# Delta-rule phase: order of conv taps, norms, solve rows, projections and grams inside an iteration

## The reference, cut to what matters

```
x = x + attn_b(layernorm(x))

q, k, v = silu(causal_conv(h @ q_w)), silu(causal_conv(h @ k_w)), silu(causal_conv(h @ v_w))   # 4 taps per channel
beta = sigmoid(h @ b_w);  g = sigmoid(h @ mix_w + mix_b + mix_bias)
q, k = l2norm(q), l2norm(k);  v = v * beta;  kb = k * beta
attn = where(strictly lower, -(kb @ k.T), 0)              # per chunk, 32 x 32
for i in 1 .. 31:  attn[i, :i] += attn[i] @ attn          # solve of a triangular system, row by row
T = attn + I;  u = T @ v;  w = T @ kb
for each chunk:                                           # the chain over the state S
    u = u - w @ S
    o = q @ S + where(lower, q @ k.T, 0) @ u
    S = S + k.T @ u
o = g * o + (1 - g) * v
o = o * rsqrt(mean(o * o) + eps) * o_norm_w
out = o @ o_w
```

## Time and profile before

| | us |
|---|---|
| three runs | 2082.21, 2083.87, 2087.22 |
| median | 2083.87 |
| the profiled execution's own time | 2075.59 |
| its span in the trace | 2073.9 |
| iterations i = 1 to 6 (2 to 5 hold all five stages, 1 no tail, 6 no tile to load) | 63.3, 68.8, 63.4, 64.8, 65.8, 60.3 |
| VectorE / TensorE / ScalarE busy, iteration 1566.7 to 1631.5 | 48.3 / 48.3 / 33.0 |

### The profile page before, as it was taken

The page is one execution under the profiler, slowest core; times in us unless marked ns, Lnnn a source line. Parts: engine busy times, 40 slices in busy tenths (PEclk is TensorE's granted clock), DMA queues, the critical chain, the costliest instruction groups (busy, mean ns, idle before and its releaser), DMA issues. The chain is left out here.

```text
span 2073.9 us, 33664 instructions
## 1 busy us (share of the span) xinstructions
PE 1227.0 (59%) x13780; PEld 588.4 (28%) x13780; DVE 1440.7 (69%) x1745; ACT 915.5 (44%) x1681; POOL 1108.7 (53%) x527
## 2 busy tenths in 40 slices
PE   4356556655555655553476464577777777637655
PEld 2112112121211212120133221244544445423322
DVE  3799899999989999999661123676697667536102
ACT  5556564746556474554122205443455444213220
POOL 1879798798979888899511001234442344440100
PEclk8676767777676777765689877777788787768877
DMA  4828183462818356281289972122212222148997
GB/s 124 190 50 193 32 198 78 124 151 52 195 28 201 74 132 133 52 190 34 79 351 373 386 292 54 31 53 63 59 40 60 66 61 64 43 120 356 368 395 275
DMA packets 195624, 301.87 MB, mean 146 GB/s; under 512 B 84176, under 2 KB 126672, under 8 KB 179088
## 3 DMA queue, kind: packets, MB, share of 16 engines
q1 hardware_dynamic: 190656, 297.26, 48.8%
q0 software_dynamic: 2304, 2.37, 0.5%
q10 hardware_dynamic: 2512, 0.10, 0.1%
HBM read 257.21 MB, written 42.47 MB: 145 GB/s over the span
## 5 line engine op out<-in xcount | busy, mean ns | idle before, releaser
L361 POOL TENSOR_TENSOR state<-dx_rep,b_rep 128x2048 f32<-128x2048 f32 x128 | 578.1, 4521 | 120.4 <-PE psum L729 93.4
L591 DVE TENSOR_TENSOR_SCAN psum<-psum,state 128x1024 f32<-128x1024 f32 x160 | 365.2, 2282 | 29.5 <-ACT psum L472 18.0
L472 ACT ACTIVATE psum<-delta_rep,a_neg 128x511 f32<-128x511 f32 x512 | 331.4, 684 | 67.7 <-DVE state L591 67.6
L729 PE MATMUL psum<-state,sel 128*32 128x512 f32 x1024 | 181.7, 812 | 199.0 <-POOL state L370 185.8
L660 PE MATMUL psum<-xt,w_in 128*128 128x512 f32 x256 | 180.2, 870 | 154.8 <-DVE x_conv L560 52.1
L591 DVE TENSOR_TENSOR_SCAN state<-psum,state 128x1024 f32<-128x1024 f32 x96 | 218.8, 2280 | 19.1 <-ACT psum L472 19.1
L370 POOL TENSOR_TENSOR state<-state,c_rep 128x1024 f32<-128x1024 f32 x96 | 225.4, 2348 | 0.6 <-DVE state L591 0.6
L598 DVE TENSOR_TENSOR state<-psum,c_rep 128x1024 f32<-128x1024 f32 x160 | 195.9, 1224 | 5.5
L856 POOL DMA_DIRECT2D moe_b<-in_w x64 | 33.0, 522 | 254.1 <-DVE moe_xt L1007 253.5
L469 ACT COPY psum<-zeros 128x2 f32<-128x2 f32 x160 | 26.2, 164 | 281.0 <-DVE state L598 276.2
L660 PEld LDWEIGHTS psum<-xt,w_in 128*128 128x128 f32 x256 | 69.1, 283 | 272.4 <-issue 124.7
(11 more groups left out here) (214 smaller groups left out, 2509.9 us busy)
## 6 DMA issues: line engine op xcount, KB each, us to landing
moe_w_set<-in_w SPq DMA_DIRECT2D x32, 4096.0 KB, 37.3
delta_rep<-delta_scratch SPq DMA_DIRECT2D x128, 256.0 KB, 5.3
dx_rep<-dx_scratch SPq DMA_DIRECT2D x128, 256.0 KB, 8.0
b_rep<-bc_scratch SPq DMA_DIRECT2D x32, 256.0 KB, 4.8
delta_scratch<-delta SPq DMA_DIRECT2D x32, 256.0 KB, 4.2
dx_scratch<-delta_x SPq DMA_DIRECT2D x32, 256.0 KB, 3.8
c_rep<-bc_scratch SPq DMA_DIRECT2D x32, 256.0 KB, 7.9
moe_x<-x_after SPq DMA_DIRECT2D x16, 512.0 KB, 10.6
```

Of the source, the lines that this page charges most:

```text
L361: nc.gpsimd.tensor_tensor(ring[q % RING][:, :, :], dx_rep[u % CHUNKS][:, :, :], free_bcast(b_rep[q // QPB % 2][:, g, :], 1, CB), ALU.mult) ...
L472: ins = nc.scalar.activation(dec[:, i, 1:], delta_rep[u % CHUNKS][:, c, 1:], ACT.Exp, scale=a_neg[:, dt * CB + c, g:g + 1])
L591: nc.vector.tensor_tensor_scan(bx if by_pool(k) else flat, flat, bx, 0.0, ALU.mult, ALU.add).then_inc(S["scan_done"], 1)
L729: ins = nc.tensor.matmul(bank[32 * c:32 * c + 32, :], sel[:, :], ring[q % RING][:, c, :], start=False, stop=(g == NG4 - 1), skip_group_che ...
```

## The change

It moves steps between slots on VectorE, ScalarE and TensorE. No instruction is added or taken away but waits; the programs of SP and GpSimd are untouched.

- The first projection of a unit and its `last_tap` leave the last slot of one iteration for the first of the next; TensorE's six projections stand in slots 0, 1, 2, 2, 4, 5.
- VectorE's taps run in pairs behind the three state copies; `bn_stats` and `bn_aggr` move from slot 3 to slot 0; `o_ms` from 3 to 2; the shift from 5 to 4. Solve rows 1 to 5, 6 to 9, 10 to 12 and 13 to 15 stand at slots 3, 5, 7 and 8. The residual add moves from 7 to 8.
- ScalarE's output and layer norms go one slot ahead, the four norms activations from slot 7 to 4; `ot_delta`, `silu`, `squares` one slot back.
- TensorE's outputs, statistics, `turn_rows` and tokens go one slot back; the grams from 12 and 14 to 13 and 14, with the masks behind each. For the first unit the grams stand ahead of the tokens (11, 12 and then 13, 14).

The core of the diff:

```diff
+        def token_slots(f):
+            return (13, 14) if f == 0 else (11, 12)
+        def gram_slots(f):
+            return (11, 12) if f == 0 else (13, 14)
...
# ScalarE
-                        if front is not None and m < 5:
-                            last_tap(f, m + 1)
-                        if tail is not None and m == 2:
+                        if front is not None and m < NT:
+                            if f == 0 and m == 0:
+                                act.wait_ge(S["conv_loaded"], 16 * 3)
+                            last_tap(f, m)
+                        if tail is not None and m == 1:
                             act.wait_ge(S["o_added"], tail + 1)
...
-                        if tail is not None and m == 4:
+                        if tail is not None and m == 3:
                             act.wait_ge(S["o_ms"], tail + 1)
...
-                        if conv is not None and m == 4:
+                        if conv is not None and m == 3:
                             act.wait_ge(S["ln_mv"], CT * (a + 1))
...
+                        if conv is not None and m == 4:
+                            act.wait_ge(S["ln_shift"], a + 1)
+                            for n_ in range(CT):
+                                ins = nc.scalar.activation(x[:, n_, :], x[:, n_, :], ACT.Identity, bias=nmr[:, n_:n_ + 1],
+                                                           scale=rstd[:, n_:n_ + 1])
+                            ins.then_inc(S["ln_done"], 1)
-                        if tail is not None and m == 5:
+                        if tail is not None and m == 6:
...
-                        if conv is not None and m == 7:
-                            act.wait_ge(S["ln_shift"], a + 1)
...
-                        if front is not None and m == 11:
-                            for n_ in range(CT):
+                        if front is not None and m in token_slots(f):
+                            for n_ in (0, 1) if m == token_slots(f)[0] else (2, 3):
...
-                        if conv is not None and m == 15:
-                            if a == 0:
-                                act.wait_ge(S["conv_loaded"], 16 * 3)
-                            last_tap(a, 0)
...
# VectorE
-                        if solve is not None and m == 0:
-                            for row in range(1, 6):
-                                solve_row(solve, row)
-                        if front is not None and m == 1:
-                            taps(f, (0, 1))
-                        if front is not None and m == 3:
-                            taps(f, (2, 3))
-                        if conv is not None and m == 3:
+                        if conv is not None and m == 0:
                             dve.wait_ge(S["x_loaded"], 64 * (a + 1))
...
-                        if tail is not None and m == 3:
+                        if tail is not None and m == 2:
                             dve.wait_ge(S["o_sq"], tail + 1)
...
-                        if solve is not None and m in (4, 5):
-                            for row in (range(6, 9) if m == 4 else range(9, 12)):
-                                solve_row(solve, row)
-                        if conv is not None and m == 5:
+                        if front is not None and m in (2, 4, 6):
+                            taps(f, (m - 2, m - 1))
+                        if conv is not None and m == 4:
                             dve.wait_ge(S["ln_rstd"], a + 1)
...
-                        if tail is not None and m == 7:
+                        if solve is not None and m in (3, 5, 7):
+                            for row in {3: range(1, 6), 5: range(6, 10), 7: range(10, 13)}[m]:
+                                solve_row(solve, row)
+                        if tail is not None and m == 8:
                             dve.wait_ge(S["res_loaded"], 64 * (tail + 1))
...
-                        if front is not None and m in (13, 14):
-                            if m == 13:
+                        if front is not None and m - 1 in gram_slots(f):
+                            pair = gram_slots(f).index(m - 1)
+                            if pair == 0:
                                 dve.wait_ge(S["lam_mask"], f + 1)
...
# TensorE
                             pe.wait_ge(S["n_read"], HS * w)
                             pe.wait_ge(S["attn_read"], HS * w)
+                            pe.wait_ge(S["tok_ready"], CT * w)
...
-                def gram(f, pair):
+                def gram(f, pair, xts):
                     feat = feats[f % COPIES]
-                    if pair == 0:
+                    if pair == 0 and f:
                         pe.wait_ge(S["tok_ready"], CT * (f + 1))
+                    elif pair == 0:
+                        pe.wait_ge(S["stat_ready"], 1)
+                        pe.wait_ge(S["gate_exp"], 1)
+                        pe.wait_ge(S["ssq_ln"], 1)
+                        pe.wait_ge(S["xt_ready"], KD * xts)
...
+                        if f == 0:
+                            pe.wait_ge(S["n_read"], HS)
+                            pe.wait_ge(S["attn_read"], HS)
...
-                            if m < 5:
-                                project(f, m + 1)
+                            for j in {0: (0,), 1: (1,), 2: (2, 3), 4: (4,), 5: (5,)}.get(m, ()):
+                                project(f, j)
...
-                        if conv is not None and m == 15:
-                            project(a, 0)
```

47 lines of the change are left out of this document (21 added, 26 removed).

## The result

| | before | changed |
|---|---|---|
| median of 4 runs, us | 2083.09 | 2114.63 |
| ratio to before, 95% interval | | 1.0147 (1.0129 to 1.0166) |
| span of the profiled execution | 2073.9 | 2115.1 |
| from the phase's first load to its last store | 598.0 | 634.7 |

The sign was forecast (+11.8), the size was not (+31.5). The profiled pair differs by more (41.2), since the profiled execution of before lay 7.5 us under its median and that of the changed kernel 2.2 above; 36.7 of it are inside the phase.

What follows compares the result with a forecast made beforehand. No engine is full; a chain through several sets the length. Four full iterations (+8.4), the one before (+3), the one after (+1.5), fill (+1.0) and last solve (-2.1) give +11.8 us: 2095.7 us, range 2078 to 2104.

Steps and rivals of the forecast that it cites:

- the start, +2.1: Head of a full iteration: VectorE's first step waits for x_delta, queued behind n_lane on SP, 2.1 us longer.
- TensorE's last stretch, -0.6: End of a full iteration: minus_vn and k_times_state run earlier, the stops stay; 0.6 us given back.
- VectorE up to the add, +1.8: VectorE, first step to residual add: 28.5 us instead of 26.7, taps paying 1.6 for GpSimd; add 3.9 late with the start.
- ScalarE's norms: ScalarE's norms, moved ahead, wait 5 to 7 us for the shift; squares 4.2 us late, gates 2.7 late.
- rival 1: TensorE's stops vanish or fall under the masks' wait, the loop through SP sets the length: -5, 2079 us; chance 0.16.
- Rival 3: TensorE idles before o's transposes, its clock falls, output products and statistics take 2 us more: +21, 2105 us; chance 0.10.
- The iteration behind the full ones, +1.5: Iteration without a tile to load: no x_delta wait or norms, but the first state copy needs k_times_u; +1.5 us (0 to 2.5).
- The one ahead of them, +3: Iteration without a tail, before the full ones: the norms' delay shows in full; +3 us (2.1 to 5).
- The first stretch: Phase start: first gram skips the tokens' transposes, -2.3; tile load +2.1, next iteration 1.2; together +1.0 us.
- The last solve's -2.1: Last solve: state copy and o_ms fit into its wait for n_lane, saving 2.1 us.
- 2: Gates late by only half; five iterations at +0.3, ends as forecast: +2, 2086 us; chance 0.22.
- 4: x_delta lands as early as n_lane and norms are ready, so the wait is filled: -10, 2074 us; chance 0.04.

Runs made afterwards that it cites:

- bn_late: The changed kernel with bn_stats and bn_aggr back at slot 3, behind the first taps, loads left in place; 2092.08 us, 1.0044.
- load_first: The changed kernel with SP issuing the next tile's four x_delta loads ahead of n_scratch and n_lane; 2082.35 us, 0.9997.
- before_first_gram: The kernel before, with only the first unit's grams put ahead of the tokens' transposes; 2087.32 us, 1.0008.

## Why the tile is later than the forecast: instruction packets

Instruction packets are the transfers of the queue that the DMA view calls "instruction". The forecast had the tile 2.1 us behind `n_lane`. In the two first iterations of the changed kernel it was so (5.9 and 5.5 us from `n_lane`'s issue to the statistics, against 3.57 + 2.1 = 5.7), in the full ones 7.0, 6.9, 8.2 and 7.6. SP's timeline shows where: the four loads take 3.26 us to issue instead of the 1.86 of the earlier trace rows,

```profile
1583.46 0.34 SPq L1342 DMA_DIRECT2D n_lane<-n_scratch  x1
1583.85 3.26 SPq L1301 DMA_DIRECT2D x_delta<-x_after  x4
```

and the DMA view from 1583 to 1585.5 has `n_lane` landing after 6.4 us instead of the 3.5 of the earlier trace rows, with a packet of the instruction queue in the same stretch:

```profile
q8 instruction: 1, 0.02, 4.5%
...
n_lane<-n_scratch SPq DMA_DIRECT2D x1, 512.0 KB, 6.4
```

In the half microsecond from 1584.5 that packet has

```profile
q8 instruction: 1, 0.02, 22.4%
```

of 16 engines' time, 0.224 x 16 x 0.5 = 1.8 us of one engine (others 1.2 to 1.4). The Trainium skill ("DMA: Bandwidth & Descriptors", Queues, rings and completion order) says that one copy is split over rings of up to 16 engines; so the engine that carries the packet would delay the whole copy, and what SP issues behind it. All eight `n_lane` transfers of each kernel, against the packets that hold an engine for 0.8 us or more ("long" below):

| | long packet begins 0.3 to 1.5 us after the issue | lands after |
|---|---|---|
| before | none of 8 | 3.4 to 3.6 |
| changed | 5 of 8 | 4.7, 5.0, 6.4, 5.4, 5.6 |
| changed, the other 3 | | 3.3, 3.4, 3.6 |

One of the other three has a short packet there, of 0.3 us, and landed after 3.4. Over all 14 kernels, 30 of 112 transfers have a long packet 0.3 to 1.6 us behind the issue: 27 landed after 4.5 to 6.8 us, three after 3.9 to 4.0. Of the other 82, 76 landed after 3.1 to 4.4 us and six after 4.9 to 5.3, five of these with one packet 3 us ahead of the issue and another 2.5 us behind it. So the link is close and not strict.

`pe_shifted` has 32 more small matmuls at the head of the phase, and nothing else:

```diff
                 pe.wait_ge(S["masks"], 4 + CT * 6)
+                for _ in range(32):
+                    nc.tensor.matmul(u_bank[0:32, 0:32], neg_ident[0:32, 0:32], neg_ident[0:32, 0:32], start=True, stop=True,
+                                     skip_group_check=True)
                 iterations(iteration)
```

> The changed kernel, and at the head of the phase 32 more small matmuls on TensorE (64 in the profile's count, half of the 128 that lie between two stops; under 1 us by themselves). In the changed kernel n_lane landed 4.7 to 6.4 us after its issue in those five iterations in which a packet of the instruction queue began within 1 us after the issue, and 3.3 to 3.6 in the other three; before, no packet began there and all eight landed in 3.4 to 3.6. Theory A (the late tile is 2.1 us of queueing behind n_lane, as forecast, and the rest are these packets, one of which holds a DMA engine for 1.2 to 1.8 us): the packets move by half their spacing, n_lane lands in 3.4 to 4 again in most iterations, and the head waits are 1 to 2 us shorter there; 4 to 8 us in all if the shift stays, 2107 to 2111. Rival (both are late for another reason): landings stay at 5 to 6, the time at 2114.

Measured: 2107.20 us, 1.0110 (1.0086 to 1.0134): 7.4 us faster than the change, although it does more. The landings moved with the packets. Two iterations that had no long one behind the issue now have one, 0.7 us behind it, and there `n_lane` takes 5.6 and 5.4 us (it was 3.4 and 3.3); in three of the full iterations the packets are 2.9 to 4.5 us behind the issue, in the fourth one is at its start, and the landings are 4.4, 3.7, 3.7 and 3.3. From the DMA view at the issue of the third full iteration, and at the first of the two late ones:

```profile
n_lane<-n_scratch SPq DMA_DIRECT2D x1, 512.0 KB, 3.7
```

```profile
n_lane<-n_scratch SPq DMA_DIRECT2D x1, 512.0 KB, 5.6
```

That a packet at the issue delays the landing is shown in so far as moving the one moved the other, both ways. The tile is another matter. In the third full iteration `n_lane` lands 2.6 us sooner than in the changed kernel, and the statistics still start 7.3 us behind its issue (8.2 there):

```profile
1576.33 0.34 SPq L1342 DMA_DIRECT2D n_lane<-n_scratch  x1
1576.71 1.85 SPq L1301 DMA_DIRECT2D x_delta<-x_after  x4
...
1583.62 1.41 DVE L1667 BATCH_NORM_STATS2 bn_stats_delta<-x_delta 128x6 f32<-128x256 f32 x4 [11.02 <-DMA x_delta<-x_after]
```

The packet has moved from the start of `n_lane` into the tile's own loads, 2.9 us behind the issue. In the mean of the full iterations the statistics start 7.3 us behind the issue of `n_lane`, against 7.4 in the changed kernel. The tile of the 48 iterations of all kernels in which it is loaded behind `n_lane` bears this out: the last of its four loads landed 5.5 to 6.5 us behind the issue of `n_lane` in the 20 that have no long packet from 0.3 to 4.5 us behind it, and 6.3 to 8.5 (median 7.3) in the 28 that have one, be `n_lane` itself late or not. So a late tile goes with a packet anywhere in the two transfers, and the forecast's 5.7 us holds where there is none.

The time fell into the theory's range (2107 to 2111), but not for its reason, that the head waits are 1 to 2 us shorter. The first steps of the full iterations moved by +2.0, +0.7, -2.7 and -1.1 us, 1.1 in all: in the first because a packet falls beside `n_scratch`, 3 us ahead of the issue, and the tile's loads land 0.6 later, in the second because these land 1.0 later. The full iterations together are 7.4 us shorter, so most of this lies behind the heads. There TensorE's stops have moved, too: those of the four full iterations sum to 10.3 us, 21.6 in the changed kernel. How much of the gain is theirs isn't told apart here; but a shift that leaves the order of the steps alone is worth 7 us in this kernel, and differences of that size between two of the kernels below can be due to it.

## The norms

`norms_late` puts ScalarE's four norms behind the squares again:

```diff
-                        if conv is not None and m == 4:
+                        if conv is not None and m == 7:
                             act.wait_ge(S["ln_shift"], a + 1)
```

> The changed kernel, but ScalarE's four norms stand behind the squares again (slot 7). Theory A (the statistics wait for the residual add, which VectorE's own queue sets; the norms' wait of some 8 us costs only the 0.9 us by which VectorE's second state copy is late): 1 us an iteration, 5 in all, about 2110. Rival: the norms' wait is on the path to the squares and gates and costs 3 us or more an iteration: 2098 or less.

Measured: 2105.89 us, 1.0102 (1.0081 to 1.0123): 8.7 us for the norms, between theory and rival. In its profile the first stretch is 3.6 us shorter, and the iteration without a tail and the full ones 1.5 each. In the full ones the gates are only 0.3 us earlier, but the residual add, and with it the rest of the solve, 1.7 us: TensorE has been idle for 3.3 to 3.9 us ahead of the statistics, and runs them at a granted clock of 0.55 to 0.69.

> Both: loads of the next tile ahead of n_scratch, and the norms behind the squares again. Theory A: the two add up, about 2080 (30 + 5 us from 2114.6). Rival: with an early tile the shift is no longer what ScalarE waits for, and the norms cost nothing: equal to the run with early loads alone.

Measured: 2075.81 us, 0.9964 (0.9950 to 0.9977). Both edits add up (6.5 us on top of the early loads), and this is the first version under the time before, by 0.4%. Its waits show what is next: TensorE waits for the residual add, which now stands behind solve rows 10 to 12, and then runs the statistics at a lower clock. The same view (stretch, length, busy, clock) for it, for the changed kernel and for before:

```profile
1591.10:1596.40 5.30, 5.30 (x16) 1.20 (x16) 5.06 (x8) 0.00 (x0) 1.82 (x1) 0.67 0.38 99
```

```profile
1620.06:1625.00 4.94, 4.94 (x18) 1.20 (x21) 4.70 (x8) 0.00 (x0) 1.46 (x1) 0.73 0.41 106
```

```profile
1593.50:1597.10 3.60, 3.58 (x18) 1.21 (x19) 3.39 (x7) 2.27 (x5) 0.00 (x0) 1.00 0.58 146
```

TensorE had been idle for 5.56, 2.70 and 1.41 us ahead of these. 1.00 is its upper level, 2.4 GHz, throughout; 0.67 and 0.73 are stretches that are in part at the lower one, 1.2 GHz. In the kernel with both edits all four full iterations are like this (0.62 to 0.69, idle for 5.4 to 5.6 us before). In the changed kernel it is only the one shown: in the other three TensorE was idle for 1.5 to 1.7 us, and the statistics run at 1.00 (as they do in one iteration of `bn_late` after 2.65 us of idle time):

```profile
1544.02:1548.50 4.48, 4.48 (x20) 1.10 (x24) 4.24 (x8) 1.05 (x2) 1.00 (x1) 1.00 0.45 117
```

## The last stretch: a gram behind a wait for the solve

`pe_front_early` takes the kernel with early loads and late norms and moves TensorE's statistics, `turn_rows`, tokens and first gram one slot ahead again.

```diff
-                            if m == 8:
+                            if m == 7:
                                 statistics(f, 2 * (tail + 1) if tail is not None else 0)
...
-            return (11, 12) if f == 0 else (13, 14)
+            return (11, 12) if f == 0 else (12, 14)
```

> The changed kernel with early loads and late norms (2075.8), and on TensorE statistics, turn_rows, tokens and first gram one slot ahead again, as in the kernel before (masks as before too). In the changed kernel the stretch from the gates to the last mask was 25.3 us in the mean of the four full iterations, against 24.1 before. Theory: the order on TensorE costs that 1.2 us an iteration, 2070. Rival: it costs nothing, since ScalarE's xt and the stops of some 128 matmuls set this stretch: 2075 to 2077. Should the first masks have saved TensorE time by standing behind the state copy, it is slower, 2080.

Measured: 2083.39 us, 0.9986 (0.9969 to 1.0003), 7.6 us slower than without it, or 4.6 by the two ratios. Neither the theory nor its rival; slower as in the last branch, but not for its reason. The gates themselves come 2 us later (43.3 instead of 41.4), because the statistics, which wait 4.79 us for the residual add, now stand in front of `k_times_state`, and the chain's `y_copy` on ScalarE in front of `stat_rows`. Four moves at once tell nothing of the gram; `changed_gram_early` and `gram_early` below move it alone.

`add_early` puts the residual add ahead of solve rows 10 to 12 (again with early loads and late norms); in the program its lines also stand ahead of those of the rows:

```diff
-                        if tail is not None and m == 8:
+                        if tail is not None and m == 7:
                             dve.wait_ge(S["res_loaded"], 64 * (tail + 1))
```

> The changed kernel with early loads and late norms (2075.8), and VectorE's residual add at slot 7 ahead of solve rows 10 to 12, where the kernel before had it, instead of behind them. In that kernel TensorE waits 5.56 us for the add in front of the statistics (iteration of 1556.5), ScalarE's squares have ended 3 us before, and the statistics' 16 matmuls take 5.30 us at a granted clock of 0.67, against 3.6 us at 1.00 before. Theory: the add is the last to come; 2.5 to 3 us earlier in the four full iterations, and up to 1.5 more if the shorter idle time leaves TensorE its clock: 2059 to 2066, faster than both kernels. Rival: the time saved is waited away later, since TensorE's stops or GpSimd's chain set the end of the iteration: 2072 to 2077.

Measured: 2079.29 us, 0.9971 (0.9952 to 0.9990), against 0.9964 without the edit: no gain, which is the rival, if 2 us above its range. The gates do come 3.5 us earlier (37.9 instead of 41.4), with the statistics at clock 1.00, and all of it is lost between gates and last mask: 28.7 us instead of 24.65. TensorE's timeline in its iteration that begins at 1552:

```profile
1605.52 0.64 PE L1759 MATMUL psum<-s_delta,feat 128*32 128x128 f32 x16 [4.27 <-DVE o_delta L1644]
1606.09 1.93 PE L1863 MATMUL psum<-feat 32*32 32x64 f32 x126
```

The first gram's inputs have been ready for some 5 us; it stands behind `q_times_state`, which waits for `read_o`, which stands on VectorE behind the whole solve. The solve ends no sooner than without the edit (`read_o` is through 53.6 us behind the last mask, 53.4 without it), so what comes earlier ahead of this point only makes the wait longer. The change had put the gram there, from slot 12 to 13.

`changed_add_early` is the same edit on the changed kernel alone.

> The changed kernel with that edit alone: the residual add ahead of solve rows 10 to 12, norms and loads left as changed. There ScalarE's squares end at 1619.74 and the add at 1619.91: held back by the norms, the squares are as late as the add. Theory: moving the add brings at most the clock of the statistics, since they still wait for the squares: 0 to 1 us an iteration, 2110 to 2115. Rival (the add was what the statistics waited for, the squares follow for another reason): as much as in the other run, 2104 or less.

Measured: 2123.11 us, 1.0189 (1.0160 to 1.0218), 8.5 us slower. Both expectations missed. It bears the reading above out: here VectorE waits up to 1.5 us for the output products in front of the add and 1.0 us behind it, the solve ends 1.8 us later (61.6 us behind the last mask instead of 59.8), `read_o` with it, and the gram behind that. The waits of TensorE in the phase, and for comparison the same group in the changed kernel:

```profile
PE psum L1759 <- DVE o_delta L1644: 55.0, 15, 6.0
```

```profile
PE psum L1759 <- DVE o_delta L1644: 47.1, 14, 6.0
```

The group holds two places of the iteration. In the last stretch, in front of the gram, the waits sum to 10.9 us in the changed kernel (1.2 to 1.7 in each full iteration, 3.6 behind them) and to 19.8 here, which is the loss; the rest of the group, in the middle of the iteration, hardly moved. In the kernel before the group is 25.7 us, and 2.0 of them, once, in a last stretch.

`changed_gram_early` and `gram_early` put only the first gram back in front of `t_times_y` and `q_times_state`, the former in the changed kernel, the latter on top of `add_early`:

```diff
-            return (11, 12) if f == 0 else (13, 14)
+            return (11, 12) if f == 0 else (12, 14)
...
-                        if front is not None and m - 1 in gram_slots(f):
-                            pair = gram_slots(f).index(m - 1)
+                        if front is not None and m in ((12, 13) if f == 0 else (13, 14)):
+                            pair = m - (12 if f == 0 else 13)
```

> The changed kernel with that edit alone. There the wait for read_o in front of the first gram is 1.15 us in the full iteration that begins at 1577.6, and the stretch from gates to last mask 1.2 us longer in the mean than before. Theory (this wait is the 1.2 us): 1 to 1.5 us in each of five iterations, 2107 to 2110. Rival (the stretch is longer for another reason): 2113 to 2116.

Measured: 2101.41 us, 1.0083 (1.0063 to 1.0104): 13.2 us faster than the change, more than the theory had. The last mask comes 24.3 us behind the gates (25.3 in the changed kernel), and 20.4 (24.1) in the iteration behind the full ones, which gets 4.2 us shorter: 7.7 us in five iterations for the theory's 5 to 7.5. The rest lies mostly ahead of the gates (46.5 us instead of 47.3), where the edit doesn't reach. What made it isn't shown; three of the full iterations no longer have a packet behind the issue of `n_lane`, which is the luck of place that `pe_shifted` shows.

> The kernel with early loads, late norms and the early residual add (2079.3), and on TensorE the first gram ahead of t_times_y and q_times_state again (slot 12), with the masks where the kernel before had them. There the gates came 4 us earlier than without the early add, and the stretch from gates to last mask was 28.7 us instead of 24.65: TensorE waited 4.27 us in q_times_state for read_o, which stands on VectorE behind the solve, with the gram queued behind it (iteration of 1552). Theory: with the gram ahead of that wait, it ends before the solve does, and the masks follow read_o at once instead of 2.7 us later; 2.5 to 4 us an iteration in four to five iterations, 2062 to 2069. Rival: the stops of TensorE take it back, since the matmuls up to the second gram's end are the same: 2076 to 2080.

Measured: 2054.41 us, 0.9867 (0.9843 to 0.9891), 24.9 us faster than `add_early` (22 by the ratios) and 28.8 faster than the kernel before. The full iterations are down to 62.9 us (66.1 before). TensorE's timeline in the iteration that begins at 1542:

```profile
1593.39 1.48 PE L1863 MATMUL psum<-feat 32*32 32x64 f32 x128 [0.73 <-ACT tok L1564]
...
1596.58 0.65 PE L1759 MATMUL psum<-s_delta,feat 128*32 128x128 f32 x16 [1.16 <-DVE o_delta L1644]
```

The gram runs as soon as the tokens are copied, and the wait for `read_o` behind it costs 1.16 us. In the last stretches of the full iterations this group's waits sum to 4.5 us instead of 19.9. A full iteration is 3.7 us shorter, inside the theory's 2.5 to 4; its range (2062 to 2069) was passed because the two beside them gained too (2.7 and 3.3 us), and the last solve and drain another 3.1. Of these 2.1 are luck of place: the last `n_lane` lands after 3.6 us, without a packet behind its issue, where it took 5.7 with one. The stops of the full iterations shrank as well, from 23.6 to 18.2 us.

## The first unit's gram alone

> The kernel before with one part of the change alone: for the first unit the grams stand ahead of the tokens' transposes. In the changed kernel the stretch from the phase's first load to the first masks' end was 4.0 us shorter than before (56.9 against 61.0). Theory: this part does that by itself, by the 4.4 us of transposes that the first gram skips: 2079 to 2080. Rival: the next unit's first projection now waits for the tokens, which gives most of it back: 2082 to 2083.

Measured: 2087.32 us, 1.0008 (0.9990 to 1.0026): no gain, the rival's side. In its profile the stretch up to the first masks is 58.7 us (61.0 before), and the next iteration 54.9 (53.4), so 0.8 is left. Of the 4.0 us that the changed kernel gains in the first stretch, this part brings 2.3; what brings the rest isn't shown.

## Why the prediction was wrong

The steps that failed are two terms of the sum for a full iteration: the start, +2.1, which measured +3.9, and TensorE's last stretch, -0.6, which measured +1.2. In the profiled pair the phase got 36.7 us longer where the sum has 11.8. Of the 24.9 us between them each of these two has some 7, the iteration behind the full ones 5.8, the way from the residual add to the gates 2.4, the iteration ahead of the full ones 2.0 and the last solve 2.0; the start of the phase gave 2.4 back. (In the medians the miss is 19.7; the profile of before was a fast one.)

**What bounds the kernel: right.** The `n_lane` wait was not the prize; it was exchanged for another.

**The start of the iteration, +2.1: the mechanism was right, the size wrong.** The wait is for `x_delta` behind `n_lane`, and it is 3.9 us longer instead of 2.1: the statistics start 7.4 us behind the issue of `n_lane`, where the forecast had 5.7. Missing were the instruction packets: I took `n_lane`'s 3.5 us and the issues' 1.86 us from a place of the trace where no packet fell. It is also the term on which most hangs: without this wait (`load_first`) the changed kernel is as fast as before, so the other losses were paid for by gains that the forecast did not have. One is seen in its timeline, the statistics that VectorE does while it waits for the state; what each is worth isn't measured.

**VectorE up to the add, +1.8: right.** It is +1.9 (5.87 - 3.94); the taps pay 1.66 us for GpSimd and the product has it back, and the second state copy waits 0.9 us, both as forecast. (The steps listed sum to 28.4 us and not 28.5, and the solve's 2.1 + 0.9 - 0.5 to 2.5 and not 2.6; neither matters.)

**ScalarE's norms: the mechanism was right, the sizes too small.** They wait 8.4 to 9.6 us where 5 to 7 were given. They cost 8.7 us in all, where 5 were expected of that run. The squares are 6.3 us late and not 4.2, most of it by the head; from them to the gates 1.0 comes back, from the residual add to the gates 0.6 where the forecast had 1.2. In one of the four full iterations the wait in front of the statistics cost TensorE its clock (0.73, 4.9 us for these matmuls instead of some 4.4). Rival 3 had this for the output products; it struck the statistics, and in the changed kernel once.

**TensorE's last stretch, -0.6: wrong, +1.2.** I had looked at what fills TensorE's idle time at the next head and not at what now stands in front of the first gram. The listing of the order ahead of the prediction shows `q_times_state` there; its wait for `read_o` in this stretch is 1.2 to 1.7 us in the full iterations, where before there was none, and with the gram ahead of it (`changed_gram_early`) the stretch is 24.3 us again (24.1 before) and the time 13.2 us shorter. The 1.2 itself is only good to a microsecond: in `before_first_gram`, whose full iterations have the order of before, the same stretch is 25.2 us, with more of the stops in it. The claim that this stretch begins with the tokens held only for the kernel before. The stops did stay (31.9 us in the phase in front of the gram, `k_times_u` and `attn_times_u`, against 33.8), so the step against rival 1 held here; but not because the matmuls are the same in number, for in `pe_shifted` they are the same but for 32 and the stops of the full iterations are half as long.

**The ends.** The iteration behind the full ones, +1.5, was +7.3; in `changed_gram_early` 4.2 of these are gone. The one ahead of them, +3, was +5.0. The first stretch gained 4.0, where the 2.3 gained and 2.1 for the tile's load made 0.2, and the next iteration gave 2.6 back instead of 1.2. The last solve's -2.1 did not come: the state copy and `o_ms` were through at 1798.0, but solve row 1 began at 1801.18, 3.18 us later, for an `n_lane` that took 5.6 us to land beside a packet.

**Rivals.** 1, 2 and 4 fell. Rival 3's end of +21 was the nearest, by another sum.

## What to carry to other kernels

Before a step is moved to the head of a queue, follow its input back through the queue that issues it: here one line on SP, ahead of two other transfers, was worth 32 us and turned the loss into none, while in the kernel before it brought nothing. In front of work that is ready, put no step that waits for another engine's queue; `read_o` stood at the end of the longest queue of all. And when two things are late together, moving one (the add) can make the time worse by delaying what the other waits for. Last, 32 matmuls that do nothing were worth 7 us here; before a gain of this size is put down to an edit of the order, see in the profile that it lies where the edit is.

## What was not expected of the hardware

A transfer of 512 KB that lands in 3.1 to 4.4 us takes mostly 4.5 to 6.8 us when a packet of the instruction queue (0.02 MB, 0.8 to 1.9 us of one DMA engine) begins 0.3 to 1.6 us behind its issue, and in the changed kernel the four issues behind it took 2.8 to 3.3 us instead of 1.86. 32 small matmuls, which do nothing, moved those packets, halved TensorE's stops in the full iterations and made the kernel 7.4 us faster. The stops go with the packets: between 1503 and 1624 us before, and 1503 and 1650 us in the changed kernel, the twelve of 1.0 us and more lie multiples of 126 to 128 matmuls apart, and at each a packet begins between 1.8 us ahead and 0.1 us behind. The Trainium skill ("Runtime: NRT & Kernel Launch", Instruction fetch mechanics) calls the cost of crossing a block mostly hidden; here it is not, neither for TensorE (these stops last 1.0 to 2.5 us) nor for the transfers beside it.
